# One core, four chained layers: instruction order rewritten on all queues, one PSUM placement moved, unread products added

## The chip, the cores and the metric

One core of one Trainium2 chip. The metric is the device time of one execution in microseconds, the median of three runs. A core has TensorE (matrix products), VectorE (DVE), ScalarE (ACT) and GpSimd (POOL), each with its own instruction queue, and SyncE (SP), whose queue here only issues transfers. The queues run in order and meet at semaphores.

## The reference

64 batches of 128 rows of 128 features go through four residual layers. `ctx` has 77 context rows of 256 features for each batch.

```python
x = x + cross_attention(ctx, layernorm(x), mask)      # 8 heads, keys = ctx[:, :128], values = ctx[:, 128:]
x = x + sign_ffn(layernorm(x), k0, k1, k2, s0, s1, s2)  # [x, -x] -> 512 -> 512 -> 128, weights +1 or -1, relu
x = x + rms_project_depool(layernorm(x), ctx, lens, W_in, b_in, g_res, g_init)
x = x + mixture(layernorm(x), W, b, Wg, bg)             # 8 experts, all computed; the two best are weighed
```

In the third layer the row norm of `x` is projected by `W_in`; to each row a decayed sum of the normalised context rows is added, picked by a running count of marks that come from `lens` ("the counts").

## The kernel before

The 64 batches are 16 groups, g0 to g15, of four batches (512 columns). Each group passes through stages named by their layer: `a_` attention, `b_` the sign network, `c_` projection and depool, `d_` gates, `e_` experts. Every engine's queue is a list of such calls written out by hand, in which three or four groups are under way at a time; a call waits on the semaphores of what it reads, and everything behind it on its queue waits with it.

TensorE's part of a group:
- `a_turn_rows` (transposes of the normalised rows, L2358), `a_scores` in two halves (L2378 the mask, L2385 the products; 64 row-tiled passes in all), `a_turn_maxima` (L2397 for g0 and g1, L2393 else), `a_weights` in two halves (scores turned, less the maxima: L2422 and L2426 for g0 and g1, L2417 else), `a_values` (L2439, column-tiled), `a_turn_out` (eight transposes, L2447)
- `b_turns` (only g0 and g1; others are turned by a transposing DMA), `b_layer` 1 to 4 (L2476) and 5 to 8 (L2483), `b_last` (L2494)
- `c_turns`, `c_project` (L2514, L2515), `d_turns`, `d_gate_scores` (L2532; L2534 for g15), `d_gate_turn` (L2540), `e_experts` for each of four batches (L2547, float32: each of the two products is two passes)

VectorE takes the row statistics (`a_stats`, `b_stats`, ...; L1127, L1136), the maxima (`a_highest` in two halves, L1162), the division (`a_weigh`), the low halves of the float16 pairs (`b_low`, L1227), the choice of experts (`d_gates`, `d_top`) and the weighing (`e_weigh`, L1305; `e_accumulate` in the last two groups, L1323). ScalarE normalises (L1815), copies the turned tiles, takes the exponents (`a_exponent`, L1866) and the high halves (`b_high`). GpSimd makes the inverse roots (`rstd`, L754 to L761; L755 is its second instruction), scales the context and adds the weighed experts. SP issues the loads and stores.

Once, at the start: `make_ends`, `mark_ends` (VectorE, L1098 to L1107) and `count_ends` (TensorE, 64 small products into bank 7, L2353) turn `lens` into counts; `counts_out` and `counts_in` move them through memory, and `make_plug` needs the result. `make_halves` (L1061) and `make_weights` (L1066 to L1068) on VectorE turn the sign bytes `k_u`, which ScalarE's queue loads together with `s_raw`, into float16 weights. `load_weights` loads the expert weights `w_T` and `last_row` (which lies in the tile `weighed`), 592 KB each.

PSUM has eight banks. `pa(g)` gives the attention of g1 banks 4 to 7 and that of all other groups banks 0 to 3. `b_layer` works in banks 4 and 5 by turns. Turns, projection and gates use 6 and 7. `a_values` and `a_turn_out` write the first two banks of `pa(g)`; so for g1 they share 4 and 5 with `b_layer`:

```python
a_scores(g[3], 0, (a_mT, g[2]), (a_q2T, g[3]))
a_values(g[1], (b_lo, g[0], 5))
a_scores(g[3], 1, (a_max[0], g[3]))
a_turn_out(g[1])
a_weights(g[2], 0, (a_max[1], g[3]))
b_layer(g[0], 5, (a_att, g[1]))
```

Of the kernel before, what the change touches and what calls it, by code (L numbers as in the profile page):

```python
# [9 lines left out]
ACT = mybir.ActivationFunctionType  # L10
# [63 lines left out]
def build(nc, x, ctx, keys, values, mask, mask_turned, lens, b_attn, signs, scales, weights, gains, patch_gains, out):  # L74
# [18 lines left out]
    with es:  # L93
# [170 lines left out]
        a_mT = signal("a_mT")  # L264
# [81 lines left out]

        def pb(g, k):
            return ps[:, (0 if g.n == NG - 1 else 4) + k % 2, :]
# [98 lines left out]
        def _(sp):  # L447
# [116 lines left out]
            load_context(g[2])  # L564
            plugs_out()
            plug(g[0])
            load_keys(g[2])
            load_rows(g[4])
            plug(g[1])
            load_context(g[3])  # L570
            load_keys(g[3])
            spread_maxima(g[2])
            load_context(g[4])
            load_values(g[2])
            load_values(g[3])
            plug(g[2])
            load_context(g[5])
            load_context(g[6])
            load_rows(g[5])
# [6 lines left out]
            plug(g[4])  # L586
            b_turn(g[2])
            load_keys(g[5])
            load_values(g[5])
            spread_maxima(g[4])  # L590
            load_rows(g[7])
            load_context(g[8])
            store(g[0])
            b_turn(g[3])
            load_keys(g[6])
            load_values(g[6])
            plug(g[5])
            load_rows(g[8])
            spread_maxima(g[5])
            plug(g[6])  # L600
            load_context(g[9])
            store(g[1])
            b_turn(g[4])
            load_keys(g[7])
            load_values(g[7])
            spread_maxima(g[6])
            plug(g[7])
            load_rows(g[9])
            load_context(g[10])
# [5 lines left out]
            spread_maxima(g[7])  # L615
            load_context(g[11])
            plug(g[8])
# [13 lines left out]
            spread_maxima(g[9])  # L631
            plug(g[10])
            load_context(g[13])
            store(g[5])
            b_turn(g[8])
            load_keys(g[11])
# [3 lines left out]
            plug(g[11])  # L640
# [3 lines left out]
            load_keys(g[12])  # L644
            load_values(g[12])
# [22 lines left out]
            plug(g[15])  # L668
            store(g[10])
            b_turn(g[13])  # L670
# [13 lines left out]
        def _(pool):  # L684
# [123 lines left out]

            rstd(ln_a, g[0])
# [3 lines left out]
            a_patch_normalise(g[0])  # L813
            rstd(ln_a, g[2])
            make_signs()
            rstd(ln_a, g[3])
            a_patch_scale(g[1])
            rstd(ln_b, g[0])
            rstd(ln_a, g[4])
            make_ones()  # L820
            make_sums_zero()
# [4 lines left out]
            a_patch_normalise(g[2])  # L826
            a_patch_scale(g[3])
# [3 lines left out]
            rstd(ln_b, g[2])  # L831
            a_patch_gain(g[2])
            rstd(ln_d, g[0])
            a_patch_normalise(g[3])
            a_patch_scale(g[4])
# [3 lines left out]
            e_out(g[0], 0)  # L839
            a_patch_scale(g[5])  # L840
            e_add(g[0], 1)
# [10 lines left out]
            a_patch_scale(g[6])  # L852
            e_add(g[1], 0)
            rstd(ln_c, g[2], 1)
# [4 lines left out]
            e_out(g[1], 2)  # L859
            a_patch_gain(g[4])  # L860
            rstd(ln_d, g[2])
            a_patch_normalise(g[5])
            a_patch_scale(g[7])
            rstd(ln_b, g[4])
            e_add(g[1], 3)
            e_out(g[1], 3)
            rstd(ln_a, g[8])
            e_add(g[2], 0)
            rstd(ln_c, g[3], 1)
            e_out(g[2], 0)  # L870
# [11 lines left out]
            e_add(g[3], 0)  # L882
            rstd(ln_c, g[4], 1)
            e_out(g[3], 0)
            e_add(g[3], 1)
            e_out(g[3], 1)
            rstd(ln_a, g[9])
            e_add(g[3], 2)
            a_patch_gain(g[6])
            rstd(ln_d, g[4])  # L890
            e_out(g[3], 2)
            a_patch_normalise(g[7])
            rstd(ln_b, g[6])
# [2154 lines left out]
```

How the kernel before makes its waits and increments, by code:

```python
            def load_rows(g):  # L449
                if g.has(4):
                    sp.wait_ge(a_x1.sem, a_x1.of(g, back=4))
                sp.dma_start(xa[:, g.f, :], x[g.n]).then_inc(rows_in[g.f].sem, 16)
# [1 line left out]
            def load_keys(g):  # L455
                if g.has(2):
                    sp.wait_ge(a_less[1].sem, a_less[1].of(g, back=2))
                sp.dma_start(kT[:, g.p], keys[g.n]).then_inc(keys_in[g.p].sem, 16)
# [1 line left out]
            def spread_maxima(g):  # L461
                sp.wait_ge(a_mT.sem, a_mT.of(g))
                if g.has(FR + 2):
                    sp.wait_ge(max_in[g.p].sem, max_in[g.p].of(turn(g), back=1))
                sp.dma_start(max_d[g.p], mq[:]).then_inc(max_out.sem, 16)
                sp.wait_ge(max_out.sem, max_out.of(g))
                sp.wait_ge(a_q2T.sem, a_q2T.of(g))
                for e, q in enumerate((qT, q2T)):
                    sp.dma_start(q[HD * (1 - e)::32, g.p, :].rearrange("r (b s) -> r b s", b=G),
                                 max_d[g.p].rearrange("(r b e) s -> e r b s", r=R, b=G)[e]).then_inc(max_in[g.p].sem, 16)
# [1 line left out]
            def b_turn(g):  # L473
                sp.wait_ge(b_lo.sem, b_lo.of(g, 1))
                if g.has(2):
                    sp.wait_ge(b_psum.sem, b_psum.of(g, FC, back=2))
                sp.dma_start_transpose(zT[:, g.p].rearrange("d part (j s) -> d (part j) s", j=G),
                                       zr[:].rearrange("s part c -> s (part c)")).then_inc(b_turned[g.p].sem, 16)
```

## Time and profile before

| | us |
|---|---|
| median of 3 runs | 516.08 (515.64 to 517.08) |
| the profiled execution | 515.66 |
| its span, first to last instruction | 513.9 |
| TensorE busy | 475.7 |
| VectorE busy | 414.2 |
| ScalarE busy | 346.1 |
| GpSimd busy | 350.2 |

The profile is of one execution. A busy time is the time in which an engine executes; overlapping weight loads of TensorE are counted apart. The page gives the clock granted to TensorE as a share of 2.4 GHz: 1.00, or 0.50 for 1.2 GHz. A time in brackets behind a row is the engine's idle time before it and what ended it.

### The profile page before, as it was taken

The numbers are of one execution on the slowest core, as the hardware profiler recorded it, in microseconds if no ns is written. First come the engines' busy times: TensorE is split into PE (matmuls) and PEld (weight loads), VectorE is DVE, ScalarE is ACT, GpSimd is POOL, SyncE is SP. The second block draws the span as 40 slices with busy tenths as digits, with TensorE's granted clock in tenths as the row PEclk, the third lists the DMA queues.
The fourth block names the chain that finished last, engine by engine and source line by source line (L and its number), as shares of the span: only waits on it lengthen the run. The fifth ranks groups of instructions, "written<-read, shape, count | busy, mean of one in ns | idle before, by whom it ended". The sixth has DMA issues, their size and how long they took to land.

```text
span 513.9 us, 13995 instructions
## 1 busy us (share of the span) xinstructions
PE 475.7 (93%) x4986; PEld 293.1 (57%) x4986; DVE 414.2 (81%) x1400; ACT 346.1 (67%) x746; POOL 350.2 (68%) x595
## 2 busy tenths in 40 slices
PE   2875989999999999999999999999999999989976
PEld 2662565646665565656665564756566565555533
DVE  6675778797987889788988889788888877677885
ACT  2367788888785877857785877678766756654211
POOL 6448535796867599785878589785858484574752
PEclk9988999999999999999999999999999999999978
DMA  6461621223221321223132222212021101010000
GB/s 198 95 200 30 156 80 35 72 69 80 57 68 36 88 74 55 72 57 92 40 85 55 70 74 65 63 51 72 11 69 35 42 6 42 3 20 22 1 30 34
DMA packets 30206, 32.12 MB, mean 63 GB/s; under 512 B 18776, under 2 KB 21048, under 8 KB 30136
## 3 DMA queue, kind: packets, MB, share of 16 engines
q1 hardware_dynamic: 29688, 30.74, 22.1%
q8 instruction: 40, 0.66, 0.5%
q10 hardware_dynamic: 448, 0.48, 0.3%
q14 instruction: 30, 0.25, 0.2%
HBM read 23.02 MB, written 4.47 MB: 54 GB/s over the span
## 4 chain that ended last, share of the span: by engine, by line
PE 74%; DVE 9%; ACT 6%; POOL 6%; issue 4%; DMA 1%; SPq 0%; DVEq 0%; POOLq 0%; ACTq 0%
PE ps L2547 18%; PE ps L2483 17%; PE ps L2494 6%; PE ps L2439 5%; PE ps L2417 5%; PE ps L2476 5%; PE ps L2358 4%; PE ps L2385 3%; PE ps L2514 2%; ACT xn L1815 2%; PE ps L2515 2%; PE ps L2447 2%; POOL rs L759 2%; ACT prT L1866 1%; DVE st L1127 1%
## 5 line engine op out<-in xcount | busy, mean ns | idle before, releaser
L794 POOL TENSOR_TENSOR sum<-weighed 128x512 f32<-128x512 f32 x59 | 76.5, 1297 | 74.5 <-DVE weighed L1305 74.5
L2547 PE MATMUL ps<-w_T,y4T 128*128 128x512 f32 x256 | 125.5, 616 | 0.3 <-DVE weighed L1305 0.3
L2483 PE MATMUL ps<-h,w 128*128 128x512 f16 x512 | 120.2, 380 | 0.0
L1227 DVE SCALAR_TENSOR_TENSOR h<-ps,h 128x512 f16<-128x512 f32 x128 | 85.4, 683 | 27.4 <-ACT h L1904 26.3
L1904 ACT ACTIVATE h<-ps 128x512 f16<-128x512 f32 x128 | 73.7, 591 | 37.8 <-PE ps L2483 31.3
L1305 DVE TENSOR_TENSOR weighed<-ps,wgt 128x1024 f32<-128x1024 f32 x59 | 71.8, 1218 | 26.3 <-PE ps L2547 25.7
L1866 ACT ACTIVATE prT<-ps,maskT 77x1024 f32<-77x1024 f32 x64 | 67.4, 1103 | 21.1 <-PE ps L2417 15.8
L2483 PEld LDWEIGHTS ps<-h,w 128*128 128x128 f16 x512 | 48.5, 98 | 56.4 <-issue 7.1
L759 POOL TENSOR_TENSOR rs<-ve,neg_half 128x4 f32<-128x4 f32 x64 | 66.3, 1035 | 8.7
L2547 PEld LDWEIGHTS ps<-w_T,y4T 128*128 128x128 f32 x256 | 45.1, 192 | 42.3 <-issue 40.3
L1162 DVE TENSOR_REDUCE mx<-ps 128x8 f32<-128x616 f32 x64 | 47.8, 788 | 6.0 <-PE ps L2385 6.0
L1815 ACT ACTIVATE xn<-xd,nm,rs 128x128 f32<-128x128 f32 x64 | 26.4, 482 | 32.8 <-POOL nm L761 32.8
L796 POOL TENSOR_TENSOR sum<-sum 128x256 f32<-128x256 f32 x59 | 44.1, 747 | 4.6
L754 POOL TENSOR_TENSOR ve<-mv,eps 128x4 f32<-128x4 f32 x64 | 18.4, 287 | 40.9 <-DVE mv L1136 40.5
L2358 PE MATMUL ps<-ident,xn 128*128 128x128 f32 x200 | 33.5, 294 | 11.4 <-ACT xn L1815 6.6
L2358 PEld LDWEIGHTS ps<-ident,xn 128*128 128x128 f32 x200 | 24.1, 149 | 25.2 <-DVE weighed L1305 8.5
L2476 PE MATMUL ps<-zT,w 128*128 128x512 f16 x128 | 35.9, 387 | 2.1 <-DVE h L1227 1.4
L2494 PEld LDWEIGHTS ps<-w,h 128*128 128x128 f16 x512 | 29.7, 98 | 7.2 <-issue 5.5
L2439 PE MATMUL ps<-prT,vx 77*32 77x128 f32 x1024 | 31.3, 274 | 2.1 <-issue 1.3
L2439 PEld LDWEIGHTS ps<-prT,vx 77*32 77x32 f32 x1024 | 27.1, 110 | 9.8 <-issue 8.7
L798 POOL TENSOR_TENSOR sum<-sum 128x128 f32<-128x128 f32 x59 | 28.4, 482 | 4.6
L2494 PE MATMUL ps<-w,h 128*128 128x128 f16 x512 | 31.2, 219 | 0.4 <-DVE h L1227 0.4
(168 smaller groups left out, 896.8 us busy)
## 6 DMA issues: line engine op xcount, KB each, us to landing
cx<-in_ctx SPq DMA_DIRECT2D x16, 320.0 KB, 3.2
vx<-in_values SPq DMA_DIRECT2D x16, 320.0 KB, 3.1
kT<-in_keys SPq DMA_DIRECT2D x16, 308.0 KB, 2.9
xa<-in_x SPq DMA_DIRECT2D x16, 256.0 KB, 2.7
out_x<-xo SPq DMA_DIRECT2D x16, 256.0 KB, 2.1
plugs<-plug_d SPq DMA_DIRECT2D x16, 77.0 KB
w_T<-in_weights SPq DMA_DIRECT2D x1, 592.0 KB, 4.3
weighed<-in_weights SPq DMA_DIRECT2D x1, 592.0 KB, 5.9
```

The source lines that it names most:

```text
L759: nc.gpsimd.tensor_tensor(rs[n][:, p], ve[n][:, p], neg_half[:], ALU.pow).then_inc(ln.rs.sem, 1)
L794: nc.gpsimd.tensor_tensor(sum4[:], both[:, 0:4 * D], both[:, 4 * D:8 * D], ALU.add).then_inc(c_sum4.sem, 1)
L1227: last = nc.vector.scalar_tensor_tensor(h[:, 1, (k - 1) % FC, :], src, 0.0, h[:, 0, (k - 1) % FC, :], ALU.max, ALU.subtract)
L1305: nc.vector.tensor_tensor(weighed[:, place(g, j), :].rearrange("p (e d) -> p e d", e=E), pm(g, j).rearrange("p b (e d) -> p (b e) d", d=D) ...
L1866: last = nc.scalar.activation(prT[:, 2 * q + j].rearrange("k (r e) s -> k r (e s)", r=R), pa(g)[0:NK, :, j * HR * S:(j + 1) * HR * S], ACT ...
L1904: last = nc.scalar.activation(h[:, 0, (k - 1) % FC, :], src, ACT.Relu)
L2358: last = pe.transpose(dst[:, j * rows:(j + 1) * rows], src(j), ident[0:rows, 0:rows])
L2439: last = pe.matmul(pa(g)[32 * i:32 * i + 32, at // 4, (at % 4) * S:(at % 4 + 1) * S], vx[0:NK, g.p, j, h, :], prT[:, j, h, :], start=True, ...
L2476: last = pe.matmul(pb(g, k), w1[:, c * 128:(c + 1) * 128], zT[:, g.p, part, :], start=(part == 0), stop=(part == 1))
L2483: last = pe.matmul(pb(g, k), w2[:, i, c * 128:(c + 1) * 128], h1[:, g.p, part, i, :], start=(i == 0 and part == 0), stop=(i == FC - 1 and ...
L2494: last = pe.matmul(pb(g, k)[:, j * D:(j + 1) * D], h2[:, part, i, j * S:(j + 1) * S], w3[:, i, :], start=(i == 0 and part == 0), stop=(i = ...
L2547: last = pe.matmul(pm(g, j)[:, half, :], y4T[:, g.p, j * S:(j + 1) * S], w_moeT[:, half * 512:(half + 1) * 512], start=True, stop=True)
```

## The change

Four things:
- The order of the calls is written anew on all five queues, from the first instruction on; what each call computes is as before, but for the two points below.
- On SP, `load_weights` and `load_gains` go ahead of `counts_out`; so do two more context tiles.
- `a_values`, `a_turn_out` and what reads them (`a_out_copy`, `a_weigh`) use a new function `pv(g)`: banks 6 and 7 for g1, banks 0 and 1 for the others. The waits on the readers of these banks change with it.
- `unread` issues products of two identity matrices (204 columns, bfloat16) whose results nothing reads: 16 into the free end of bank 7 behind `a_turn_rows(g[2])`, after a wait for the second maxima of g1, and 26 into bank 0 ahead of `d_turns(g[15])`.

```diff
+        def pv(g):
+            return ps[:, 6:8] if g.n == 1 else ps[:, 0:2]
...
+            def unread(bank, first, n, *readers):
+
+                free(*readers)
+                for _ in range(n):
+                    pe.matmul(ps[:, bank, first:first + 204].rearrange("p (a c) -> p a c", a=2), ident_bf[:],
+                              ident_bf[:, 0:102].unsqueeze(1).to_broadcast([128, 2, 102]), start=True, stop=True)
...
 # SP
             load_rows(g[1])
             mask_rows()
+            load_context(g[0])
             load_keys(g[1])
+            load_context(g[1])
             load_rows(g[2])
-            load_context(g[0])
+            load_context(g[2])
+            load_values(g[0])
             load_rows(g[3])
-            load_values(g[0])
-            load_context(g[1])
+            load_weights()
+            load_gains()
             counts_out()
+            load_values(g[1])
+            load_context(g[4])
             counts_in()
-            load_weights()
-            load_values(g[1])
-            load_gains()
-            load_context(g[2])
+            load_context(g[3])
+            load_keys(g[2])
             plugs_out()
...
 # VectorE
+            make_counters()
             a_stats(g[0])
             make_mask()
+            make_key_mask()
+            a_stats(g[1])
             make_ends()
-            make_counters()
-            a_stats(g[1])
+            make_halves()
             mark_ends()
+            a_highest(g[0], 0)
             a_normalise(g[1])
-            a_highest(g[0], 0)
-            make_halves()
-            make_key_mask()
             a_highest(g[0], 1)
             a_split_maxima(g[0])
+            take_counts()
             a_stats(g[2])
-            take_counts()
+            a_stats(g[3])
             a_highest(g[1], 0)
-            a_stats(g[3])
             a_normalise(g[2])
             make_plug()
             a_highest(g[1], 1)
-            a_normalise(g[3])
             a_split_maxima(g[1])
+            make_weights()
             a_weigh(g[0])
             a_residual(g[0])
             b_stats(g[0])
-            make_weights()
...
 # ScalarE
             a_queries(g[0])
-            a_maxima(g[0])
             a_squares(g[0])
             a_queries(g[1])
+            a_squares(g[1])
+            a_maxima(g[0])
             a_exponent(g[0], 0)
+            a_squares(g[2])
             a_exponent(g[0], 1)
-            a_squares(g[1])
             a_out_copy(g[0])
             a_maxima(g[1])
             a_queries(g[2])
             a_exponent(g[1], 0)
+            a_decays(g[0])
+            a_exponent(g[1], 1)
             b_normalise(g[0])
-            a_exponent(g[1], 1)
+            a_maxima(g[2])
             b_high(g[0], 0)
...
 # TensorE
             a_scores(g[0], 0)
+            count_ends()
+            a_scores(g[0], 1, (a_max[0], g[0]))
             a_turn_rows(g[1])
-            a_scores(g[0], 1, (a_max[0], g[0]))
-            count_ends()
             a_turn_maxima(g[0], (a_max[1], g[0]))
...
             a_values(g[0])
+            a_turn_rows(g[2])
+            unread(7, 308, 16, (a_max[1], g[1]))
             a_turn_maxima(g[1], (a_max[1], g[1]))
-            a_turn_rows(g[2])
             a_turn_out(g[0])
...
+            a_turn_rows(g[3], (a_max[1], g[2]))
+            a_turn_maxima(g[2])
             b_turns(g[0], (a_prT[1], g[1]))
-            a_turn_maxima(g[2], (a_max[1], g[2]))
-            a_turn_rows(g[3])
             b_layer(g[0], 1)
             b_layer(g[0], 2)
+            a_scores(g[3], 0, (a_mT, g[2]), (a_q2T, g[3]))
+            a_values(g[1])
+            a_scores(g[3], 1, (a_max[0], g[3]))
             b_layer(g[0], 3)
             b_layer(g[0], 4)
-            a_scores(g[3], 0, (a_mT, g[2]), (a_q2T, g[3]))
-            a_values(g[1], (b_lo, g[0], 5))
-            a_scores(g[3], 1, (a_max[0], g[3]))
             a_turn_out(g[1])
             a_weights(g[2], 0, (a_max[1], g[3]))
-            b_layer(g[0], 5, (a_att, g[1]))
+            b_layer(g[0], 5)
...
             e_experts(g[14], 3, (c_weighed, g[14], 1))
+            unread(0, 0, 26)
             d_turns(g[15])
```

GpSimd's list begins with `make_ones`, and `rstd(ln_b, g[0])` stands ahead of `make_sums_zero`. In the rest of the diff calls change places with near neighbours, some tens on each compute queue; in the groups g0, g1, g5 and g6 `e_experts(·, 3)` moves from behind `a_scores(·, 0)` to ahead of it, directly behind `b_layer` 5.

## Rows read from the trace of the kernel before

**Rows 1.** Page: busy time, granted clock by slice, a costly group
```profile
PE 475.7 (93%) x4986; PEld 293.1 (57%) x4986; DVE 414.2 (81%) x1400; ACT 346.1 (67%) x746; POOL 350.2 (68%) x595
...
PEclk9988999999999999999999999999999999999978
...
L2483 PE MATMUL ps<-h,w 128*128 128x512 f16 x512 | 120.2, 380 | 0.0
```

**Rows 2.** TensorE by stretch: length, busy, granted clock, DMA share, GB/s
```profile
0.00:90.00 90.00, 66.91 (x980) 0.96 0.42 113
90.00:410.00 320.00, 316.95 (x3359) 1.00 0.23 62
...
492.00:514.00 22.00, 13.35 (x47) 0.79 0.07 25
```

**Rows 3.** DMA issues by tile, last number us to landing; one issue
```profile
weighed<-in_weights SPq DMA_DIRECT2D x1, 592.0 KB, 5.9
...
s_raw<-in_scales ACTq DMA_DIRECT2D x1, 1.5 KB, 5.2
...
7.31 0.44 ACTq L1799 DMA_DIRECT2D s_raw<-in_scales  x1
```

**Rows 4.** Timeline 8 to 19 us: start, us, engine, line, operation
```profile
7.98 0.19 DVE L1098 CAST ends_i<-ps 77x64 int32<-77x64 f32 x1
...
8.57 1.12 PE L2358 MATMUL ps<-ident,xn 128*128 128x128 f32 x4 [2.14 <-ACT xn L1815]
...
9.98 0.68 DVE L1107 TENSOR_TENSOR within<-ends_f,expert 77x512 bf16<-77x512 f32 x1
...
12.06 1.49 DVE L1162 TENSOR_REDUCE mx<-ps 128x8 f32<-128x616 f32 x2
...
13.48 0.67 DVE L1061 TENSOR_TENSOR sum<-k_u 128x512 f32<-128x512 uint8 x1
...
17.71 0.27 PE L2397 MATMUL ps<-ident_bf,mxb 128*128 128x128 bf16 x1 [0.95 <-issue]
...
18.35 0.72 PE L2422 MATMUL ps<-qT,kT 32*77 32x128 f32 x8 [0.37 <-ACT mT L1856]
```

**Rows 5.** Timeline 20 to 44 us
```profile
20.88 2.11 ACT L1866 ACTIVATE prT<-ps,maskT 77x1024 f32<-77x1024 f32 x2 [0.53 <-PE ps L2426]
...
36.61 1.34 DVE L1067 TENSOR_SCALAR w<-k_u,s_sgn 128x2048 f16<-128x2048 uint8 x1
...
36.71 1.63 POOL L755 TENSOR_TENSOR mm<-mv,minus_one 128x4 f32<-128x4 f32 x1
...
43.44 0.81 PE L2358 MATMUL ps<-ident,xn 128*128 128x128 f32 x4 [2.85 <-ACT prT L1866]
```

**Rows 6.** TensorE in the stretch from the first `b_turns` to the first `b_layer` 5
```profile
43.40:56.50 13.10, 10.47 (x162) 0.87 0.35 90
```

**Rows 7.** Timeline: the same eight transposes (`a_turn_out`) in two groups
```profile
31.24 1.92 PE L2447 MATMUL ps<-ident,oT 128*128 128x128 f32 x8
...
54.19 1.09 PE L2447 MATMUL ps<-ident,oT 128*128 128x128 f32 x8 [0.37 <-ACT oT L1884]
```

**Rows 8.** Chain of work that ended last: the expert product after two neighbours
```profile
193.15 1.72 PE ps L2547 x4
...
250.95 1.91 PE ps L2547 x4
```

**Rows 9.** Timeline of the end
```profile
494.75 1.12 PE L2358 MATMUL ps<-ident,xn 128*128 128x128 f32 x4 [2.74 <-ACT xn L1815]
...
496.57 1.50 DVE L1323 SCALAR_TENSOR_TENSOR xo<-ps,wgt,xo 128x128 f32<-128x128 f32 x4
...
496.64 1.84 PE L2534 MATMUL ps<-w_T,y4T 128*128 128x8 f32 x8 [0.78 <-ACT y4T L1921]
...
498.34 8.53 PE L2547 MATMUL ps<-w_T,y4T 128*128 128x512 f32 x16
...
505.24 0.35 DVE L1323 SCALAR_TENSOR_TENSOR xo<-ps,wgt,xd 128x128 f32<-128x128 f32 x1 [2.21 <-PE ps L2547]
```

More of the change, by code:

```diff
@@ L1961, in _ @@
             a_exponent(g[1], 0)
+            a_decays(g[0])
+            a_exponent(g[1], 1)
             b_normalise(g[0])
-            a_exponent(g[1], 1)
+            a_maxima(g[2])
             b_high(g[0], 0)
-            a_squares(g[2])
+            a_queries(g[3])
             b_high(g[0], 1)
             b_high(g[0], 2)
-            a_maxima(g[2])
-            a_queries(g[3])
+            a_normalise(g[4])
+            a_out_copy(g[1])
             b_high(g[0], 3)
             b_high(g[0], 4)
-            a_decays(g[0])
-            a_normalise(g[4])
-            a_out_copy(g[1])
             a_squares(g[3])
@@ L2042, in _ @@
             b_high(g[3], 4)
+            a_normalise(g[7])
+            a_maxima(g[5])
             a_queries(g[6])
-            a_maxima(g[5])
-            a_decays(g[4])
             b_high(g[3], 5)
@@ L2071, in _ @@
             d_normalise(g[3])
-            a_squares(g[9])
+            a_decays(g[6])
+            b_high(g[4], 6)
             d_turned(g[3])
-            b_high(g[4], 6)
             b_high(g[4], 7)
@@ L2080, in _ @@
             d_gate_exp(g[3])
-            a_decays(g[6])
             a_exponent(g[6], 0)
+            a_squares(g[9])
             a_exponent(g[6], 1)
@@ L2129, in _ @@
             a_exponent(g[8], 0)
-            a_squares(g[11])
             a_exponent(g[8], 1)
@@ L2139, in _ @@
             a_queries(g[10])
+            a_normalise(g[11])
             a_maxima(g[9])
-            a_normalise(g[11])
+            a_squares(g[11])
             b_high(g[7], 5)
@@ L2145, in _ @@
             d_turned(g[6])
-            a_decays(g[9])
             b_high(g[7], 7)
@@ L2152, in _ @@
             d_gate_exp(g[6])
+            a_decays(g[9])
             a_exponent(g[9], 0)
@@ L2167, in _ @@
             d_normalise(g[7])
-            a_decays(g[10])
+            a_squares(g[13])
+            d_turned(g[7])
             b_high(g[8], 6)
-            d_turned(g[7])
             b_high(g[8], 7)
@@ L2177, in _ @@
             a_exponent(g[10], 0)
-            a_squares(g[13])
             a_exponent(g[10], 1)
+            a_decays(g[10])
             b_high(g[9], 1)
@@ L2281, in _ @@
             b_high(g[13], 5)
-            a_decays(g[15])
             b_high(g[13], 6)
@@ L2630, in _ @@
             b_layer(g[2], 3)
+            a_turn_rows(g[5])
             b_layer(g[2], 4)
@@ L2665, in _ @@
             b_layer(g[3], 7)
+            a_scores(g[6], 1, (a_max[0], g[6]))
             d_gate_scores(g[2])
-            a_scores(g[6], 1, (a_max[0], g[6]))
+            b_layer(g[3], 8)
             d_gate_turn(g[2])
-            b_layer(g[3], 8)
             a_weights(g[5], 0, (a_max[1], g[6]))
             e_experts(g[2], 0, (c_gd, g[2]))
+            a_weights(g[5], 1, (a_prT[0], g[5]))
             b_last(g[3])
-            a_weights(g[5], 1, (a_prT[0], g[5]))
             e_experts(g[2], 1, (c_weighed, g[2], 1))
```

346 lines of the change are left out of this document (172 added, 174 removed).

## The prediction

> **What bounds the kernel now.** I read the busy times first: TensorE is busy for 475.7 of the 513.9 us, VectorE for 414.2, and the other two compute engines for about two thirds [rows 1]. Then TensorE by stretches. Between 90 and 410 us it is busy for 316.95 of 320 us: the order of the work there can win 3 us at most, and the work itself is not cut. In the first 90 us it is busy for only 66.91, in the last 22 us for only 13.35, and in both at a lower clock [rows 2]. So the change is decided at the two ends, where TensorE waits for chains that run through the other engines. The third view is the timeline of these two stretches, and the fourth the chain that ended last, for two neighbouring steps of the steady part.
>
> **The clock.** The eight transposes of `a_turn_out` take 1.92 us at 31.2 us and 1.09 us at 54.2 [rows 7]; at half clock such work takes nearly twice as long. Four transposes at 8.57 us take 1.12 us [rows 4], exactly as four do at 494.75, where the clock is at its lower level [rows 9], though the page's clock line shows 9 for that early slice [rows 1]. So I take TensorE to run at 1.2 GHz from the start until the first dense work, whatever that line says. The Trainium skill ("TensorE: Matmul & The Clock Gate", What's actually happening) says that the throttled state is the default and activity releases it; the durations agree, the clock line does not. By the line, nothing in the first 26 us could get faster with denser work; by the rule, it can.
>
> **The start, step 1: VectorE waits for the signs.** `make_halves` stood behind the first `a_highest` at 13.48 us [rows 4]. Now it stands before `mark_ends` and before that `a_highest`, and waits for both sign transfers. The later of them was issued at 7.31 us and took 5.2 us to land [rows 3]: 12.5 us. Neither the ACT order before it nor the load is much changed, so I keep 12.5. Queued behind it: `make_halves` 0.67, to 13.2; `mark_ends`, which took from 7.98 to 10.66, so 2.7, to 15.9 [rows 4]; `a_highest(g0, 0)` 1.5, which began at 12.06 and now begins at 15.9. On TensorE `count_ends` now stands before `a_scores(g0, 1)` and waits for `mark_ends`. From the begin of that `a_highest` to the first `a_turn_maxima` were 17.71 - 12.06 = 5.65 us; the new order takes about 0.4 more (the counts are ahead of the scores, 1.8 us, but overlap the reduction), so 22.0. ScalarE then still has `a_squares(g1)` in front of `a_maxima(g0)`, because `a_queries(g1)` waits for `a_turn_rows(g1)`, which is now behind both scores; that is about 0.6 more. The first `a_weights` starts at 23.2 instead of 18.35 [rows 4]: **+4.85 us**. The bounds: if the signs have landed by 9.2 us, when VectorE reaches them, `mark_ends` ends at 12.5, where `a_highest` waits for the scores anyway, and the loss is 1.9; if they land 1 us later than before, it is 5.9.
>
> **Weights ahead of the counts.** The two weight transfers, the gains and more context rows enter SP's queue before `counts_out`. One weight transfer took 5.9 us [rows 3]. They are issued near 10 us, while the counts exist only after 22, so they are through by then: nothing. `values(g1)` and a context tile now stand ahead of `counts_in`; the marks come back by about 29 instead of 24 us, and `make_plug` is reached at about 29: nothing, but with no cover left, 1 us later costs 1 us in `a_highest(g1, 1)`.
>
> **Step 2: from the first `a_weights` to the first `b_turns`.** Before this took 43.44 - 18.35 = 25.1 us [rows 4, 5]. The chain is weights, exponents (2.1 each half [rows 5]), values, turn out, weights and exponents of g1, then the ScalarE normalise and `b_turns`. Three things change. The stretch of TensorE work that begins at 23.2 has no long hole, so the clock should be up before the second half of the weights (2.5 us at half, 1.45 at full): -1.05. The 16 unread products stand behind `a_turn_rows(g2)`; 512 columns take 120.2/512 = 0.235 us [rows 1], so 204 take 0.09 and sixteen 1.5 us, up to twice that at half clock. They fall where the turned maxima are awaited, cover that hole and let `a_turn_out` run in 1.0 instead of 1.92 us [rows 7]; they themselves push the turn by about 1 us at full clock, so the net is nil, or +1.5 if the clock is down. `make_weights` moves ahead of `a_weigh(g0)` into a wait of VectorE. That frees the step in which GpSimd's L755 took 1.63 us, begun beside VectorE's L1067 of 1.34 [rows 5]; but `b_normalise(g0)` now stands behind both exponents of g1, and that sets the time. `a_decays(g0)` stands in the same row but runs while TensorE makes the second weights. Together I count 22.55 us: `b_turns` at 45.75, **-2.5 us** (bounds: 0 with the clock down, -3.5).
>
> The Trainium skill ("SBUF — State Buffer", Who interferes with whom) lets a two-port VectorE instruction lock GpSimd out until it ends; the 1.63 us agree with it. By that rule alone the move would be worth 1.4 us; by the new ScalarE order it is worth nothing by itself.
>
> **Step 3: the banks.** From `b_turns(g0)` to `b_layer(g0, 5)` were 13.1 us, in which TensorE was busy for 10.47 at a mean clock of 0.87 [rows 6]. g1's values went to banks 4 and 5, where `b_layer` works too, and waited for `b_low` 4; in banks 6 and 7 they go ahead of `b_layer` 3 and 4, into the hole between layers. The row turn of g3 and the maxima turn of g2, some 0.75 us at full clock, are now in front of `b_turns`. Without holes (2.63), with those taken out and the half clock's excess of about 1.9 gone, 7.8 us would be left; the chain ScalarE-VectorE of layers 1, 2, 3 and the two reductions of g3 between them makes it about 9.7. **-3.4 us** (bounds -5.3 and -1.5). So `b_layer(g0, 5)` starts at 55.4 instead of 56.5: +4.85 - 2.5 - 3.4 = **-1.05 us**. From there to 75 us the TensorE order is almost as before: nothing.
>
> **The steady part.** Some 60 neighbours change places on all queues. With TensorE busy for 99% it can win 3 us and lose about as much; of it I can price one pattern. In g0, g1, g5 and g6 `e_experts(·, 3)` moves from behind `a_scores` to behind `b_layer` 5. That product takes 1.72 us behind a layer and 1.91 behind row-tiled work [rows 8]; the next layer pays back half of it. Four times 0.1: **-0.4 us** (bounds -2 and +1.5).
>
> **The end.** After the last products of g14 TensorE stood idle for 2.74 us and met `d_turns(g15)` at 494.75 with the clock down; four transposes took 1.12, the gate scores 1.84, and the 16 passes of the experts 8.53 instead of 16 x 0.43 = 6.9 [rows 8, 9]. The 26 unread products take 26 x 0.09 = 2.4 us and fit into the 2.74. With the clock held the turn takes 0.66, the scores about 0.9, and the first three experts are ready at 502.2 instead of 505.2, where VectorE starts `e_accumulate(g15, 2)` [rows 9]. VectorE itself is busy with g14 until 498.07 [rows 9], so its gates begin there and not at 497.0; with 3.25 us of `d_top` and 1.23 of `e_weigh` it is free at 502.6. So **-2.6 us**. If the clock drops all the same within the gaps of the g15 chain it is -0.9; the least is 0.
>
> **Sum.** -1.05 - 0.4 - 2.6 = -4.05. The profiled execution took 515.66, so 511.6 us; the median of the three runs is 0.42 above it: 512.0.
>
> **Rivals.**
> - *The wait for the signs is not there* (they land early, or the rest overlaps it). The start then wins 3 us more: 509.0. For it: the later transfer is tiny, and its landing is known only from one execution. Against: 5.2 us. Chance 0.15.
> - *The clock falls at the end anyway.* After the unread products TensorE meets gaps again, behind the turn and behind the scores of g15. The end wins 0.9 or less: 513.7 to 514.6. The clock fell also at the hole before `b_turns` at 43.4 us [rows 5, 6]. By the skill's page on TensorE, an idle stretch brings the lower level back; that rule speaks against a filler that ends before the gaps do. Chance 0.20, of which 0.08 is within 0.3%.
> - *The late start is carried through* (slower): `b_layer(g0, 5)` starts at 61 because ScalarE's order, with both exponents of g1 ahead of `b_normalise`, gives nothing back. Then +4.85 - 2.6: 518.3. It decides from a first `b_layer` 5 later than 60.6. Chance 0.10.
> - *The order is worth nothing*: what one swap wins the next loses, as TensorE was full, and the start comes out 1.5 us late: 515 to 516.5. Chance 0.13, of which 0.10 within 0.3%.
>
> **The numbers.** The forecast (510.5 to 513.8) has 0.42. A difference of 0.3%, 1.5 us, is what a measurement of this kernel can tell from none. Faster: 0.42 + 0.15 + 0.12 + 0.03 = 0.72; same 0.08 + 0.10 = 0.18; slower 0.10. The range takes in the early signs with a steady part 1 us better, 508.0, and up to the start 3 us late with the clock lost at the end, 516.8.
>
> **What would show it.** VectorE's L1061 beginning near 12.5 with an idle time before it; the first `a_weights` at 23; `b_turns` near 46; the first `b_layer` 5 at 55 to 56; TensorE at full clock from 494 to 505 and the four transposes of g15 in 0.66 us; the first L1323 of `e_accumulate(g15, 2)` near 501 instead of 505.24. The prediction is wrong if the first weights start before 20 or after 25, if the clock line shows a fall near 490, or if the stretch from 90 to 410 moves by over 2 us.

## The result: slower, by 0.9%

| | before | after |
|---|---|---|
| median of 20 executions each, taken together | 517.1 (514.87 to 519.81) | 522.54 (517.99 to 528.03) |
| ratio, with its 95% interval | 1 | 1.0087 [1.0064, 1.011] |
| the profiled execution; its span | 515.66; 513.9 | 528.03; 526.2 |

By the ratio the change costs 4.5 us (0.87% of 517.1); the quotient of the two medians, which is formed otherwise, is 1.0105, or 5.4 us. The prediction said 512.0, with 516.8 as its upper bound. Executions of one kernel differ here by some 4 to 11 us where nine or more were taken. In the profiles TensorE's clock rises and falls at other moments in each; how much of the spread comes from that is not shown. The profiled execution of after is the longest of its 20, so the profile tells where time goes, and the ratio how much. The ratios leave out executions far above the shortest of their kernel: two of after, one of `signs_back` and six of `hole_closed`.

The page's busy times and TensorE by stretch, after (answering to [rows 1] and [rows 2]; the windows' columns are start and end, length, busy time, granted clock, DMA share, GB/s):

```profile
PE 484.3 (92%) x5028; PEld 301.3 (57%) x5028; DVE 421.7 (80%) x1400; ACT 346.2 (66%) x746; POOL 348.0 (66%) x595
...
PEclk9999599999999999999999999999999999999988
```

```profile
0.00:90.00 90.00, 62.63 (x870) 0.92 0.39 108
90.00:410.00 320.00, 314.79 (x3328) 1.00 0.24 62
...
492.00:514.00 22.00, 20.28 (x95) 0.92 0.04 13
```

The first 90 us hold less work than before (62.63 us busy instead of 66.91) at a lower clock (0.92 instead of 0.96): most of the loss is there. The 5 in the clock's line is the slice from 52.6 us, a new stretch at half clock. The third window is no longer the same work, since everything in it is some 13 us later.

The transfers, after (columns as in [rows 3]), and the timeline up to the first weights (answering to [rows 4]):

```profile
s_raw<-in_scales ACTq DMA_DIRECT2D x1, 1.5 KB, 6.9
```

```profile
7.23 0.44 ACTq L1802 DMA_DIRECT2D s_raw<-in_scales  x1
...
14.08 1.04 POOL L778 TENSOR_TENSOR hp<-cx,rk 77x512 f32<-77x512 f32 x1
14.14 1.52 DVE L1064 TENSOR_TENSOR sum<-k_u 128x512 f32<-128x512 uint8 x1 [5.30 <-DMA s_raw<-in_scales]
...
17.55 0.68 DVE L1110 TENSOR_TENSOR within<-ends_f,expert 77x512 bf16<-77x512 f32 x1
18.16 1.49 DVE L1165 TENSOR_REDUCE mx<-ps 128x8 f32<-128x616 f32 x2
18.29 1.75 PE L2363 MATMUL ps<-within,eighth 77*16 77x8 bf16 x64 [5.74 <-DVE within L1110]
...
24.93 0.72 PE L2432 MATMUL ps<-qT,kT 32*77 32x128 f32 x8 [0.57 <-ACT mT L1859]
```

VectorE stands still for 5.30 us, released by the transfer of `s_raw`, and `make_halves` and `mark_ends` behind it hand the delay to TensorE, which waits 5.74 us for `within`. The first half of g0's scores is done by then; the second half stands in TensorE's queue behind the counts that need `within`. The maxima begin at 18.16 instead of 12.06, the first weights at 24.93 instead of 18.35 [rows 4].

From there to the first `b_layer` 5 (answering to [rows 5] to [rows 7]), and the two longest waits of TensorE in the head beside the very first (us in all, times, longest):

```profile
34.37 3.64 PE L2449 MATMUL ps<-prT,vx 77*32 77x128 f32 x64 [0.97 <-issue]
...
38.85 2.93 PE L2355 MATMUL ps<-ident_bf 128*128 128x204 bf16 x16
...
41.67 1.54 PE L2457 MATMUL ps<-ident,oT 128*128 128x128 f32 x8
...
47.69 3.13 DVE L1154 TENSOR_SCALAR xn<-xa,mv,rs 128x128 f32<-128x128 f32 x4
...
48.34 2.40 POOL L725 TENSOR_TENSOR w_T<-w_T,weighed 127x1024 f32<-127x1024 f32 x1
...
52.30 0.66 PE L2368 MATMUL ps<-ident,xn 128*128 128x128 f32 x4 [3.51 <-DVE mx L1165]
...
52.90 1.01 PE L2368 MATMUL ps<-ident,xn 128*128 128x128 f32 x4
...
55.42 1.86 PE L2486 MATMUL ps<-zT,w 128*128 128x512 f16 x4 [1.50 <-DVE zT L1227]
...
58.61 3.64 PE L2449 MATMUL ps<-prT,vx 77*32 77x128 f32 x64
...
67.93 7.14 PE L2493 MATMUL ps<-h,w 128*128 128x512 f16 x32
```

```profile
PE ps L2363 <- DVE within L1110: 5.7, 1, 5.7
...
PE ps L2368 <- DVE mx L1165: 3.5, 1, 3.5
```

The 64 passes of the values take 3.64 us in both groups, against 1.96 at full clock in other runs below: the clock is down from the start until about 42 us (the unread products take 2.93 instead of 1.56, the transposes behind them 1.54, between 1.04 and 1.97), and again from 52.9 to 66.6 by the clock's records. Between the two lies the second wait, 3.51 us, ahead of `a_turn_rows(g3)`; `b_turns(g0)` stands behind that at 52.90. `b_layer(g0, 5)` comes at 67.93 instead of 56.50.

The end (answering to [rows 9]):

```profile
505.19 2.44 PE L2355 MATMUL ps<-ident_bf 128*128 128x204 bf16 x26
...
508.10 0.66 PE L2368 MATMUL ps<-ident,xn 128*128 128x128 f32 x4 [0.47 <-ACT xn L1818]
...
509.53 1.13 PE L2544 MATMUL ps<-w_T,y4T 128*128 128x8 f32 x8 [0.78 <-ACT y4T L1924]
...
510.51 8.71 PE L2557 MATMUL ps<-w_T,y4T 128*128 128x512 f32 x16
```

The unread products take the 2.44 us foreseen, and the turn of g15 runs at full clock (0.66). In this execution the clock falls after it, at 510.3 us for 3.4 us, and the 16 passes take 8.71.

Three sections split the span of a profile: up to the first `b_layer` 5; from there to the start of VectorE's last L1253 (L1250 before), which makes the rows of g15; and from there to the end. Before: 56.50, 432.54, 24.86. After: 67.93, 434.47, 23.80. So +11.4, +1.9 and -1.1 in this execution.

### The profile page after: what moved, and what is told of

Read it like the earlier page. It is cut to its first block and busy times, and to the rows that moved or that the text cites. A ratio compares the mean times of both kernels' runs of the same rounds, so it can differ in the third digit from the quotient of the medians.

```text
span 526.2 us, 14078 instructions
## 1 busy us (share of the span) xinstructions
PE 484.3 (92%) x5028; PEld 301.3 (57%) x5028; DVE 421.7 (80%) x1400; ACT 346.2 (66%) x746; POOL 348.0 (66%) x595
## 5 line engine op out<-in xcount | busy, mean ns | idle before, releaser
L1308 DVE TENSOR_TENSOR weighed<-ps,wgt 128x1024 f32<-128x1024 f32 x59 | 71.9, 1218 | 27.6 <-PE ps L2557 26.9
L757 POOL TENSOR_TENSOR ve<-mv,eps 128x4 f32<-128x4 f32 x64 | 16.6, 260 | 48.6 <-DVE mv L1139 48.3
L799 POOL TENSOR_TENSOR sum<-sum 128x256 f32<-128x256 f32 x59 | 45.3, 768 | 4.6
L2449 PE MATMUL ps<-prT,vx 77*32 77x128 f32 x1024 | 34.6, 292 | 1.5 <-issue 1.5
L2449 PEld LDWEIGHTS ps<-prT,vx 77*32 77x32 f32 x1024 | 29.9, 118 | 9.5 <-issue 9.3
```

Of the source, the lines that this page charges most:

```text
L1308: nc.vector.tensor_tensor(weighed[:, place(g, j), :].rearrange("p (e d) -> p e d", e=E), pm(g, j).rearrange("p b (e d) -> p (b e) d", d=D) ...
L2449: last = pe.matmul(pv(g)[32 * i:32 * i + 32, at // 4, (at % 4) * S:(at % 4 + 1) * S], vx[0:NK, g.p, j, h, :], prT[:, j, h, :], start=True, ...
```

## The experiments

All runs in one table. Ratios are to the kernel before, measured beside each (medians 517.59 for the first four runs, 517.92 for the next four, 516.9 for the last four; after had its own, 517.1). The last four columns are of one profile each: the first two are start times, the other two the lengths of the second and third section.

| | median, us | ratio [95%] | first weights | first `b_layer` 5 | to the last L1253 | to the end |
|---|---|---|---|---|---|---|
| before | 517.1 | 1 | 18.35 | 56.50 | 432.54 | 24.86 |
| after | 522.54 | 1.0087 [1.0064, 1.011] | 24.93 | 67.93 | 434.47 | 23.80 |
| `signs_back` | 518.83 | 1.0026 [0.9996, 1.0057] | 20.13 | 59.55 | 434.58 | 22.17 |
| `no_first_unread` | 522.84 | 1.0121 [1.0095, 1.0147] | 23.81 | 64.73 | 433.77 | 22.10 |
| `old_head_new_rest` | 515.74 | 0.997 [0.9948, 0.9992] | 18.27 | 57.80 | 433.58 | 22.12 |
| `new_head_old_rest` | 521.82 | 1.0085 [1.0053, 1.0118] | 23.25 | 63.30 | 432.31 | 25.39 |
| `hole_closed` | 519.87 | 0.9954 [0.9913, 0.9994], of 6 of its 12 executions | 20.42 | 61.89 | 434.27 | 23.84 |
| `layers_first` | 520.84 | 1.0062 [1.0034, 1.0089] | 19.90 | 58.89 | 434.25 | 23.86 |
| `both` | 516.55 | 0.9994 [0.9962, 1.0026] | 20.13 | 57.48 | 434.67 | 22.15 |
| `end_alone` | 514.9 | 0.9951 [0.9923, 0.9978] | 18.13 | 58.41 | 432.21 | 22.18 |
| `old_signs_early` | 521.65 | 1.0088 [1.0056, 1.0121] | 22.86 | 62.38 | 432.36 | 25.06 |
| `old_rest_swapped` | 517.64 | 1.0011 [0.9987, 1.0035] | 18.96 | 57.12 | 433.49 | 25.49 |
| `end_and_start_filled` | 514.79 | 0.9961 [0.9932, 0.9989] | 18.25 | 58.66 | 432.31 | 22.13 |
| `end_and_weights_moved` | 513.02 | 0.9921 [0.9892, 0.9951] | 18.24 | 55.37 | 432.27 | 22.16 |

The theory after the result was that the wait for the signs is the loss, and that nothing behind it gives any of it back. Its rivals: the 16 unread products at half clock; the new order of the rest; the hole ahead of `a_turn_rows(g3)` and the half clock behind it.

**`signs_back`: after, with the signs where they were.**

```diff
             make_ends()
-            make_halves()
             mark_ends()
             a_highest(g[0], 0)
+            make_halves()
```

> The changed kernel, with make_halves moved on VectorE from ahead of mark_ends to behind the first a_highest. Theory 1 (VectorE waits 5.3 us for the signs, with the counts and the first maxima behind it): L1064 starts without idle time before it, the first a_weights starts near 19 us instead of 24.93, and the time falls by 4 to 6 us against the changed kernel, to at or below the kernel before (0.99 to 1.00 of it). Rival (the late start is absorbed by waits that come after it, and the loss lies elsewhere): the first weights come earlier, the time stays within 1.5 us of the changed kernel, 1.008 of the kernel before.

The ratio falls from 1.0087 to 1.0026, and the intervals are apart: 3.2 us of the 4.5 are this one call, less than the 4 to 6 expected. The timeline of this kernel:

```profile
12.67 1.51 DVE L1165 TENSOR_REDUCE mx<-ps 128x8 f32<-128x616 f32 x2
14.09 0.68 DVE L1064 TENSOR_TENSOR sum<-k_u 128x512 f32<-128x512 uint8 x1
...
20.13 0.73 PE L2432 MATMUL ps<-qT,kT 32*77 32x128 f32 x8 [0.87 <-ACT mT L1859]
...
39.43 3.13 DVE L1154 TENSOR_SCALAR xn<-xa,mv,rs 128x128 f32<-128x128 f32 x4
40.08 2.40 POOL L725 TENSOR_TENSOR w_T<-w_T,weighed 127x1024 f32<-127x1024 f32 x1
...
42.49 1.49 DVE L1165 TENSOR_REDUCE mx<-ps 128x8 f32<-128x616 f32 x2
44.04 1.11 PE L2368 MATMUL ps<-ident,xn 128*128 128x128 f32 x4 [3.51 <-DVE mx L1165]
...
50.91 3.64 PE L2449 MATMUL ps<-prT,vx 77*32 77x128 f32 x64
```

The idle time before L1064 is gone. The first weights still come 1.8 us later than in the kernel before (20.13 - 18.35), which is what the prediction gave as the loss if the signs were there in time, 1.9. The hole ahead of `a_turn_rows(g3)` is the same 3.51 us, followed by 13.65 us at half clock. So there is a second loss in the new head: this kernel has the gain of the end in it (below, 0.49%) and is still not faster.

**`no_first_unread`: after, without the 16 products.**

```diff
-            unread(7, 308, 16, (a_max[1], g[1]))
```

> The changed kernel without the 16 unread products behind a_turn_rows(g2). Theory 2 (at half clock they take 2.9 us and stand in front of the turned maxima and of a_turn_out, whose input was ready at 39.1): a_turn_out(g0) starts near 39.2 instead of 41.67, the time falls by 1.5 to 2.5 us against the changed kernel. Rival (they bring the clock up and pay for themselves): a_turn_out takes 1.9 us instead of 1.54, what follows is at half clock for longer, and the time is the same or up to 1.5 us higher.

The time does not fall: 1.0121 against 1.0087. The intervals overlap, the two were measured in different sessions, and the quotients of the medians are alike (1.0101 and 1.0105), so that the products are worth something here is not shown. The rival that they are the loss falls. Its mechanism is in the profile all the same:

```profile
38.03 1.97 PE L2457 MATMUL ps<-ident,oT 128*128 128x128 f32 x8
```

The turn starts 14.2 us behind the first weights instead of 16.7 in after, and `b_turns` 25.9 us behind them instead of 28.0. At half clock the products do stand in the way, by some 2 us in this pair of profiles; the time of the whole kernel does not show it.

**`old_head_new_rest` and `new_head_old_rest`.** Each queue is cut where it reaches the same call of both orders (SP at `load_rows(g[5])`, GpSimd at `rstd(ln_b, g[1])`, VectorE at `c_stats(g[0])`, ScalarE at `a_exponent(g[2], 1)`, TensorE at `b_last(g[0])`). The first kernel has the order of before up to there, with g1's values in banks 4 and 5, and the order of after behind it, with the 26 products; the second has the head of after, with its 16 products and banks 6 and 7, and the order of before behind it.

> All five queues in the order of the kernel before up to the last layer of g0's sign network (some 66 us), with g1's values in banks 4 and 5 as before, then the remaining calls in the order of the changed kernel, its 26 unread products at the end included, the 16 at the start not. Theory 1 (the loss is in the head): 1 to 3 us below the kernel before, from the end. Rival (the loss is in the swaps of the rest): 3 to 5 us above it, 1.006 to 1.01.

> The changed kernel's order up to the same place, with its banks for g1 and its 16 unread products, then the remaining calls in the order of the kernel before and nothing unread at the end. Theory 1 (the loss is in the head): 5 to 7 us above the kernel before, 1.010 to 1.014, thus slower than the changed kernel by what its end gains (1 us). Rival (the loss is in the rest): within 1.5 us of the kernel before.

0.997 and 1.0085: the loss is in the head, 4.4 us by the second kernel and 6.0 us between after and the first. The second was expected at 1.010 to 1.014, above after by what the end gains, and it is not: the two halves together would make 1.0055, and after has 1.0087. The intervals allow for this difference of 1.6 us, but sums of such ratios are no better than that. The second one's timeline shows the giving back at its best, with the clock up early:

```profile
32.70 1.95 PE L2449 MATMUL ps<-prT,vx 77*32 77x128 f32 x64 [1.05 <-issue]
...
35.08 1.56 PE L2355 MATMUL ps<-ident_bf 128*128 128x204 bf16 x16
...
36.53 1.04 PE L2457 MATMUL ps<-ident,oT 128*128 128x128 f32 x8
...
44.53 1.64 ACT L1818 ACTIVATE xn<-xb,nm,rs 128x128 f32<-128x128 f32 x4
...
46.91 1.12 PE L2368 MATMUL ps<-ident,xn 128*128 128x128 f32 x4 [3.63 <-DVE mx L1165]
...
48.03 1.06 PE L2368 MATMUL ps<-ident,xn 128*128 128x128 f32 x4
```

Values, products and turn all run at full clock, the turn in 1.04 us, as forecast. The rows that `b_turns` needs are there at 46.17 (44.53 + 1.64), 22.9 us behind the first weights, close to the 22.55 of the prediction. Yet `b_turns` stands at 48.03, 24.8 us behind them, and before it took 25.1: the gain of step 2 goes into the wait for the maxima, a hole of 3.63 us, and the turns of g3 and of the maxima behind it.

**`hole_closed`, `layers_first`, `both`.** Three kernels on top of `signs_back`. The first moves `a_normalise(g3)` on VectorE (L1154) out from between the two maxima of g2:

```diff
             a_highest(g[1], 1)
+            a_normalise(g[3])
             a_split_maxima(g[1])
...
             a_highest(g[2], 0)
-            a_normalise(g[3])
             a_highest(g[2], 1)
```

The second puts `b_layer` 3 and 4 of g0 ahead of the scores of g3 and the values of g1 on TensorE, with `b_high` and `b_low` to match; the third does both.

```diff
             b_layer(g[0], 2)
+            b_layer(g[0], 3)
+            b_layer(g[0], 4)
             a_scores(g[3], 0, (a_mT, g[2]), (a_q2T, g[3]))
             a_values(g[1])
             a_scores(g[3], 1, (a_max[0], g[3]))
-            b_layer(g[0], 3)
-            b_layer(g[0], 4)
```

> signs_back, with a_normalise(g3) on VectorE moved from between the two maxima of g2 back to behind a_highest(g1, 1), where the kernel before has it. In signs_back it took 3.13 us beside GpSimd's L725 (2.40 us), a_highest(g2, 1) began at 42.49, TensorE waited 3.51 us for it, and its clock then stood at half for 13.65 us. Theory 3 (this stretched step makes the hole, and the hole the half clock): a_highest(g2, 1) starts near 40.5, the longest wait of TensorE between 36 and 48 us is under 2.5 us, the half-clock stretch is gone or under 7 us, b_layer(g0, 5) starts near 55 to 56 instead of 59.55, and the time falls 2.5 to 4 us below signs_back. Rival (b_turns waits for ScalarE's b_normalise until 43.6 anyway, so the hole only moves): b_layer 5 moves by less than 1.5 us and the half clock stays.

> signs_back, with b_layer(g0, 3 and 4), and their b_high and b_low, ahead of the scores and values of g3 and g1 as in the kernel before; g1's values stay in banks 6 and 7. Theory 4 (at half clock the full-array layers bring the clock back, the row- and column-tiled scores and values do not): the half-clock stretch after the hole is 3.4 or 6.8 us instead of 13.65, a_values(g1) takes 1.96 instead of 3.64 us, b_layer 5 starts at 57 to 58. Rival (the length of the half-clock stretch has to do with the hole alone): it stays 13.65 us and b_layer 5 starts at 60 or later, since the layers no longer have other work between them.

> hole_closed and layers_first together. By theories 3 and 4 the head is as fast as or faster than that of the kernel before: b_layer 5 at 55 to 57, and with the end's 2.5 us won and 1.5 us lost in the new order of the rest the time is 0.995 to 1.000 of the kernel before. If both fall, it stays with signs_back, 1.003.

`hole_closed` does shorten the wait, from 3.5 to 1.6 us, but its profile has 13.65 us at half clock all the same, and `b_layer` 5 comes at 61.89 instead of the expected 55 to 56. Its 12 executions reach from 512.53 to 523.76 us. The ratio, 0.9954, leaves out the six above 521 us and can't be used; the medians of all executions are 519.87 against 517.92. `layers_first` is no faster than `signs_back` (1.0062), though its stretch at half clock is 10.24 us instead of 13.65: that the order of the layers sets how long the clock stays down, and that this costs the time, is not borne out. Together they come to 0.9994, within what was expected, against 1.0026 for `signs_back`; the intervals overlap, so the gain is not shown. In `both` the same place reads:

```profile
42.62 1.11 PE L2368 MATMUL ps<-ident,xn 128*128 128x128 f32 x4 [1.64 <-DVE mx L1165]
```

**`old_signs_early`: before, with nothing but the signs' call moved ahead.**

```diff
+            make_halves()
             mark_ends()
             a_normalise(g[1])
             a_highest(g[0], 0)
-            make_halves()
```

> The kernel before with one call moved on VectorE: make_halves ahead of mark_ends, as in the changed kernel. Theory 1 (the wait for the signs alone delays the first maxima by some 4 us, and the head passes that on): the first a_weights starts near 23 instead of 18.35 us, and the time rises by 3 to 5 us, 1.006 to 1.010. Rival (only the changed head's other calls make it hurt): under 1.5 us.

1.0088 [1.0056, 1.0121], as expected: the wait alone, in an otherwise untouched kernel, costs as much as the whole change.

```profile
11.86 0.77 DVE L1061 TENSOR_TENSOR sum<-k_u 128x512 f32<-128x512 uint8 x1 [2.39 <-DMA s_raw<-in_scales]
...
16.57 1.49 DVE L1162 TENSOR_REDUCE mx<-ps 128x8 f32<-128x616 f32 x2
...
22.86 0.73 PE L2422 MATMUL ps<-qT,kT 32*77 32x128 f32 x8 [0.37 <-ACT mT L1856]
```

VectorE idles for 2.39 us, and `mark_ends` begins behind L1061, at 12.6 instead of 7.98 [rows 4]. That moves the maxima by 4.51 us (16.57 - 12.06) and the first weights by 4.51 (22.86 - 18.35). The time grows by 4.5 by the ratio (0.88% of 516.9; 2.9 to 6.3 by its interval), and the medians are 4.75 apart. Within that uncertainty, what is lost ahead of the first maxima comes out at the end undiminished.

**`old_rest_swapped`: the order of after behind the old head, without unread products.** It is `old_head_new_rest` less this line:

```diff
-            unread(0, 0, 26)
```

> old_head_new_rest without the 26 unread products: the kernel before up to g0's last layer, then the changed kernel's order alone. Theory 6 (the new order of the rest costs what the profiles show between the first b_layer 5 and the xd of g15, 433.6 to 434.7 us against 432.2 to 432.5): 1 to 2 us slower than the kernel before, 1.002 to 1.004. Rival (that difference is the spread of single executions): within 1 us, 1.000.

1.0011 [0.9987, 1.0035]: nothing that can be told from 1, and below the expected 1.002 to 1.004. In the profiles, the second section is 433.5 to 434.7 us in all eight kernels with the new order of the rest and 432.2 to 432.5 in the six with the old one, so 1 to 2.5 us worse, never better.

**`end_alone`, `end_and_start_filled`, `end_and_weights_moved`: parts that could pay, on the old order.** The first adds only the 26 products ahead of `d_turns(g15)`. The second adds the 16 behind `a_values(g0)` as well. The third has the 26 and moves `make_weights` on VectorE ahead of `a_weigh(g0)`:

```diff
             a_split_maxima(g[1])
+            make_weights()
             a_weigh(g[0])
...
             b_stats(g[0])
-            make_weights()
```

> The kernel before with the 26 unread products ahead of d_turns(g15) and nothing else. Theory 5 (they hold the clock over the wait for g15's rows): the four transposes take 0.66 instead of 1.12 us, 16 expert passes about 6.9 instead of 8.5, and the stretch from the xd of g15 to the end falls from 24.86 to 22.1 to 22.2 us as in three other runs: 2.5 us less, 0.995. Rival (in most executions the clock falls anyway, as in the profile of the changed kernel): 1 us or less, 0.998 to 1.000. The old order of the rest should also show 1 to 2 us less from b_layer 5 to that xd than the new.

> end_alone with the 16 unread products too, between a_values(g0) and a_turn_maxima(g1) of the old order. Theory (as the run without them says, 1.012 against 1.009: they raise the clock for the turns and weights behind them): 0.5 to 1.5 us below end_alone, 0.993. Rival (in the old head the hole is only 0.6 us, and at half clock they stand in front of the maxima for 2 us): 0.5 to 2 us above end_alone.

> end_alone with make_weights moved on VectorE into the wait ahead of a_weigh(g0), as in the changed kernel, the ScalarE order left as it was (b_normalise(g0) ahead of the second exponents of g1). GpSimd's L755 should take 0.2 instead of 1.63 us, b_normalise(g0) start 1.5 us earlier, and so the second exponents and b_turns: 1 to 1.5 us below end_alone, 0.992 to 0.993, and a shorter hole ahead of b_turns. Rival (the exponents are then bound by TensorE's second weights, which end at 38.3): 0.5 us or less.

The 26 products alone are worth 0.49% (2.5 us), as expected. The 16 add nothing in the old head (0.9961, where 0.993 was expected). With `make_weights` moved the ratio is 0.9921, the lowest of all, as expected; its interval overlaps with that of `end_alone`. Its timeline around the freed inverse roots, and its end:

```profile
36.45 0.20 POOL L755 TENSOR_TENSOR mm<-mv,minus_one 128x4 f32<-128x4 f32 x1
...
42.45 0.66 PE L2365 MATMUL ps<-ident,xn 128*128 128x128 f32 x4 [1.55 <-ACT prT L1866]
...
490.43 2.44 PE L2352 MATMUL ps<-ident_bf 128*128 128x204 bf16 x26
...
493.36 0.66 PE L2365 MATMUL ps<-ident,xn 128*128 128x128 f32 x4 [0.49 <-ACT xn L1815]
...
494.79 1.03 PE L2541 MATMUL ps<-w_T,y4T 128*128 128x8 f32 x8 [0.78 <-ACT y4T L1921]
...
495.68 7.11 PE L2554 MATMUL ps<-w_T,y4T 128*128 128x512 f32 x16
...
501.17 0.35 DVE L1323 SCALAR_TENSOR_TENSOR xo<-ps,wgt,xd 128x128 f32<-128x128 f32 x1
```

L755 takes 0.20 us instead of 1.63, the idle time ahead of `b_turns` is 1.55 instead of 2.85, and `b_turns` starts 1.0 us earlier [rows 5]. At the end the clock holds: 0.66, 1.03 and 7.11 us instead of 1.12, 1.84 and 8.53 [rows 9].

## Why the prediction was wrong, by its steps

**The start (+4.85 us): right, and the largest part of the loss.** The wait, its releaser and what is queued behind it were as told. In the profile the first weights come 6.58 us later (24.93 - 18.35), above the upper bound of 5.9: L1064 began at 14.14 instead of 12.5, since `s_raw` landed after 6.9 us instead of 5.2, and took 1.52 us instead of 0.67, begun beside GpSimd's L778. The landing is no constant: in `no_first_unread` and `new_head_old_rest` L1064 started at 13.01 and 12.43, and the first weights at 23.81 and 23.25, where the prediction had 23.2.

**Step 2 (-2.5 us, `b_turns` at 45.75): failed.** The only term of it with a price was -1.05 us, for the clock being up before the second half of the weights; the rest of the 2.5 us had none. In the three profiles with the signs early (after, `no_first_unread`, `new_head_old_rest`) all eight groups of the two halves (L2432) took 0.67 to 0.73 us, which is half clock; full clock came by 43.2, 40.3 and 32.7 us. In after the step took 28.0 us (52.90 - 24.93) instead of 25.1. In `signs_back` the second half did run at full clock (0.41 to 0.46 us a group), and the step still took 25.0 (45.16 - 20.13): nothing gained with the premise granted.

The step left out the order in front of `b_turns`. The maxima of g2 on VectorE release `a_turn_rows(g3)`, which now stands ahead of `b_turns`, and `a_normalise(g3)` had been put between them. The prediction had that turn and the turn of the maxima as "some 0.75 us", in step 3, gave them no wait, and did not add them to step 2. In `new_head_old_rest` this came to 1.9 us behind the end of the normalise (48.03 - 46.17). `a_normalise(g3)` took 1.11 us in `both`, where it starts at 30.05, and 3.13 beside GpSimd's L725 of 2.40. The Trainium skill ("SBUF — State Buffer", Who interferes with whom) says that a VectorE instruction in a two-port mode and a GpSimd instruction contend for a shared pair of ports, that whichever starts first has it for the whole instruction, and that the other is blocked; here the four instructions end at 50.82, right behind L725 at 50.74, and the trace agrees with that rule. The prediction had used the same rule for one pair of instructions and not looked for the new pairs that the order makes.

**Step 3 (-3.4 us, 9.7 us from `b_turns` to `b_layer` 5): failed.** It took 15.0 us in after, 15.3 in `new_head_old_rest`, 14.4 in `signs_back`, 13.7 in `both`; before 13.06. Two of its terms are answered by rows. The first is the 0.75 us for the turns of g3 and of the maxima, taken out of this stretch. Before, they stood in the wait between `b_turns` and the first layer, and moving them only made that wait longer, 1.50 us in after instead of this:

```profile
45.76 1.74 PE L2476 MATMUL ps<-zT,w 128*128 128x512 f16 x4 [0.44 <-DVE zT L1224]
```

From `b_turns` to `b_layer` 1 were 2.3 us before and 2.5 in after. The second is the half clock's excess of 1.9 us, which was to be gone. The clock was down for more of this stretch, not less: 13.65 us in after, where before had 3.4. What the clock costs here can be read from the old order. With 3.4 us of the stretch at half clock it took 12.9 to 13.1 in five profiles (before, `old_head_new_rest`, `old_signs_early`, `old_rest_swapped`, `end_and_weights_moved`), with 8.5 it took 13.8 (`end_alone`), and with 13.65 it took 15.8 (`end_and_start_filled`). The new order took 15.0 with the same 13.65, in after and in `no_first_unread`. So at an equal clock the new order is 0.8 us shorter, by a single profile of the old one, and not 3.4; the rest of the difference is the clock. No profile of this head has a short stretch at half clock, so what step 3 gives at full clock stays open, and so does whether the hole in front of it is what keeps the clock down for so long. That the banks 6 and 7 let the values go earlier was not tested by itself.

**The rival that held** is the third, *the late start is carried through*: it was to decide from a first `b_layer` 5 later than 60.6, and this came at 67.93, 64.73 and 63.30 in the three profiles of the head with the signs early. It was priced at 518.3, 2.2 us above before, with the whole gain of the end, and given 0.10; the measured loss of 4.5 us is twice that. Its reason was right only in part. It blamed ScalarE's order ahead of `b_normalise`, and in after that normalise does end only at 51.81, 0.5 us ahead of the turn that the maxima release at 52.30. But what came last was VectorE's maxima, with `a_normalise(g3)` between them, and behind them the clock was down.

**The new order of the rest (-0.4 us): not borne out.** 1.0011 by the ratio, 1 to 2.5 us worse in the profiles, with TensorE busy for 314.79 us between 90 and 410 instead of 316.95, 2.16 less and so just past the 2 us named as a sign of error.

**The end (-2.6 us): right.** 24.86 us became 22.1 to 22.2 in all seven profiles where the clock held, -2.7; the products alone make 0.9951. The rival that the clock falls anyway came true in after, `hole_closed` and `layers_first` (23.8 to 23.9), and then 1.0 us is left, where it was priced at 0.9.

**The 16 products (nothing): not contradicted.** In the old head they change nothing that can be told (0.9961 against 0.9951), in the new one neither (1.0087 with them, 1.0121 without, with overlapping intervals). At half clock they held `b_turns` back by some 2 us in the profiles, where the prediction allowed for 1.5. **`make_weights` (nothing by itself): argued for the new ScalarE order, and not tested there.** In the old one, beside the 26 products, the ratio went from 0.9951 to 0.9921, some 1.5 us, though the intervals overlap; in the profile L755 took 0.20 us instead of 1.63. By the Trainium skill's rule on the shared ports ("SBUF — State Buffer", Who interferes with whom) the move was to be worth 1.4 us, and these numbers agree.

**The account in ratios:** signs 0.61% (1.0087 to 1.0026); the end -0.49%; the order of the rest 0.11%; the remainder, 0.64%, some 3.3 us, is by subtraction the other rearrangement of the head. It holds only if the parts add up, and each of them is uncertain by 0.2 to 0.3%. Part of it is in front of the first weights, 1.8 us in the profile of `signs_back`. Closing the hole and bringing the layers forward may give about half of it back (1.0026 to 0.9994, with overlapping intervals). The rest stays open, and so does why the clock stays down for 10 to 17 us in one run and for three separate stretches of 3.4 us in `end_and_weights_moved`: `end_alone`, with the layers in the old order, had 13.65 us too.

## What to carry to other kernels

Where the head of a kernel is one chain, a wait put into it can be paid in full, as it was here: before counting on a later stretch to give it back, name the wait that ends last there in the new order, and give it a price. A call should not stand ahead of a chain's first reduction when it waits for a transfer that has not landed and its result is needed much later; move it behind. A rearrangement of many calls can be tested by cutting each queue at a common call: two kernels showed here which side held the loss, and one line of it, alone in the kernel before, cost as much.

## What the runs showed of the hardware

- **A small transfer can land late and unevenly.** The 1.5 KB of `s_raw`, issued behind the 448 KB of `k_u` on ScalarE's queue, took 5.2, 6.9, 5.1, 5.8 and 4.8 us in before, after, `signs_back`, `no_first_unread` and `old_signs_early`. In after `k_u` itself took 5.0, and the 19.2 KB of `mask_i`, issued on SP's queue at 1.2 us, 2.6. Whether the large transfer ahead is the reason was not tested.
- **The clock rises at another moment in each execution.** The kernel before and `end_alone` are alike up to 490 us, and yet the values of g0, at 27.8 and 27.6 us, took 1.96 us in the one and 3.64 in the other; in the new head, 3.64 in after and 1.95 in `new_head_old_rest`. The Trainium skill ("TensorE: Matmul & The Clock Gate", Part 1) says that the moment varies between runs, as what watches the engine does not start with the kernel, and gives 500 ns either way; that it varies, these rows agree, but full clock came by 32.7 us in one of two profiles of the same head and by 43.2 in the other, far more than that. One profile of such a kernel does not size a change.
- **Half clock can last through dense work.** Around a wait of 3.5 to 3.6 us it fell and stayed down for 13.65 us in after and `signs_back` and for 17.1 in `new_head_old_rest`. That the wait brings this about is not shown: `hole_closed`, with 1.6 us of wait, had 13.65 as well.
- **Unread products hold the clock up in most executions.** 26 of them, 2.44 us, filled a gap of 2.74; behind them lay gaps of 0.47 and 0.78 us, and the clock held in seven of the ten profiles that have them. In the four without them it fell at this place every time, for 6.8 us.
